# Attention between two expert layers on one core: tokens and queries of a batch made one batch ahead, the second half of the mix one score tile later and its values one batch later

## The reference

```python
x = x + 0.5 * ffn(layernorm(x))       # mixture of 16 experts, 4 chosen, and a shared one
x = x + attn(layernorm(x))            # causal attention, one head of width 128
x = x + 0.5 * ffn(layernorm(x))

# attn(x), mask -inf above the diagonal
Q = x @ Qw; K = x @ Kw; V = x @ Vw
scores = einsum('bqd,bkd->bqk', Q, K) / sqrt(128) + mask
return einsum('bqk,bkd->bqd', softmax(scores), V)
```

## Time and profile before

| | us |
|---|---|
| median of 3 runs | 779.87 (776.88 to 780.46) |
| the profiled execution | 777.23 |
| its span | 775.3 |
| first expert layer, up to the first score tile | 0 to 264 |
| attention with the start of the second layer | 264 to 545 |
| second expert layer | 545 to 775.3 |

### The profile page before, as it was taken

How to read it: one execution, slowest core, us unless ns; L and a number is a source line. 1 busy time by engine, 2 the same in 40 slices (tenths; PEclk the granted TensorE clock), 3 DMA queues, 4 the chain that set the end, 5 groups by cost and what they waited for, 6 DMA issues and landing times.

```text
span 775.3 us, 15281 instructions
## 1 busy us (share of the span) xinstructions
PE 666.4 (86%) x3395; PEld 516.1 (67%) x3395; DVE 591.0 (76%) x2650; ACT 548.4 (71%) x1138; POOL 537.9 (69%) x427
## 2 busy tenths in 40 slices
PE   5789999999999868667686676766999999999997
PEld 4567777777777646546565565655777777777775
DVE  5999898898898756564665575894888988998863
ACT  3589988988987754644545554443888889889885
POOL 3488998988998564444345353541798999989885
PEclk9999999999999968987789877787999999999999
DMA  9767577577577053434445433276388687687673
GB/s 253 164 145 169 115 163 164 123 160 157 129 163 148 1 96 69 85 68 81 80 64 83 80 57 72 47 134 138 68 172 172 144 186 166 153 177 164 148 171 92
DMA packets 129306, 97.31 MB, mean 126 GB/s; under 512 B 80992, under 2 KB 94960, under 8 KB 129264
## 3 DMA queue, kind: packets, MB, share of 16 engines
q1 hardware_dynamic: 127056, 96.24, 60.0%
q10 hardware_dynamic: 2208, 0.59, 0.4%
HBM read 72.70 MB, written 5.24 MB: 101 GB/s over the span
## 4 chain that ended last, share of the span: by engine, by line
PE 25%; DVE 16%; issue 10%; DMA 7%; ACT 6%; POOL 2%; SPq 0%; DVEq 0%; POOLq 0%; ACTq 0%
PE psum L1272 6%; DMA wb<-scratch 6%; PE psum L1274 6%; PE psum L1273 6%; DVE raw_max L1155 4%; DVE zn L1173 2%; DMA scratch<-wT 1%; PE psum L1488 1%; PE psum L1489 1%; PE psum L1490 1%; DVE s_sb L1026 1%; DVE x_sb L1185 1%; ACT s_sb L526 1%; ACT z_hi L526 1%; ACT s_sb L704 1%
## 5 line engine op out<-in xcount | busy, mean ns | idle before, releaser
L416 POOL TENSOR_TENSOR shared_r<-shared,shared_r 128x512 fp32r<-128x512 f32 x256 | 326.7, 1297 | 66.6 <-ACT shared L596 64.6
L1026 DVE SCALAR_TENSOR_TENSOR s_sb<-psum,wb 128x512 f32<-128x512 f32 x256 | 175.3, 688 | 48.8 <-PE psum L1274 21.0
L595 ACT ACTIVATE shared_r<-s_sb 128x512 fp32r<-128x512 f32 x256 | 160.0, 625 | 45.4 <-DVE s_sb L1026 43.3
L596 ACT ACTIVATE shared<-s_sb 128x512 f32<-128x512 f32 x288 | 177.9, 619 | 18.8 <-DVE s_sb L1026 18.6
L503 POOL TENSOR_TENSOR shared<-s_sb,shared 128x128 f16<-128x128 f32 (+3 forms) x64 | 81.9, 1281 | 95.7 <-ACT shared L526 95.7
L1272 PE MATMUL psum<-x_hi,w_hi 128*128 128x512 f32 x288 | 128.7, 447 | 0.4 <-DVE s_sb L1026 0.4
L704 ACT ACTIVATE s_sb<-psum,nmax 128x128 f32<-128x128 f32 (+3 forms) x64 | 47.4, 741 | 113.0 <-DVE nmax L1158 113.0
L1272 PE MATMUL psum<-shared_r,w_hi 128*128 128x512 f32 x256 | 114.6, 448 | 1.2 <-POOL shared_r L416 1.1
L1273 PE MATMUL psum<-x_lo,w_hi 128*128 128x512 f32 x288 | 115.2, 400 | 0.0
L1274 PE MATMUL psum<-x_hi,w_lo 128*128 128x512 f32 x288 | 114.8, 398 | 0.0
L1273 PE MATMUL psum<-shared_r,w_hi 128*128 128x512 f32 x256 | 101.2, 395 | 0.0
(11 more groups left out here) (182 smaller groups left out, 1425.6 us busy)
## 6 DMA issues: line engine op xcount, KB each, us to landing
wb<-scratch SPq DMA_DIRECT2D x128, 512.0 KB, 8.2
out<-x_sb SPq DMA_DIRECT2D x16, 256.0 KB, 9.9
x_sb<-in_L_attn_x SPq DMA_DIRECT2D x4, 256.0 KB, 6.0
scratch<-wT SPq DMA_DIRECT2D x32, 32.0 KB, 1.9
w_raw<-in_L_ffn_W ACTq DMA_DIRECT2D x1, 512.0 KB, 5.5
w_raw<-in_L_ffn_W SPq DMA_DIRECT2D x1, 512.0 KB, 6.5
w_raw<-shared SPq DMA_TRANSPOSE x32, 2.8
wb<-shared SPq DMA_TRANSPOSE x32, 3.9
```

Source lines behind the costliest of these rows:

```text
L416: nc.gpsimd.tensor_tensor(g_lo[:, j % RING, :], g_f[:, j % RING, :], g_hi[:, j % RING, :].bitcast(F32), ALU.subtract).then_inc(F.glo_done, 1)
L595: nc.scalar.activation(g_hi[:, j % RING, :], s_sb[:, j % RING, :], ACT.Square)
L596: nc.scalar.activation(g_f[:, j % RING, :], s_sb[:, j % RING, :], ACT.Square).then_inc(F.sq_done, 1)
L1026: ins = nc.vector.scalar_tensor_tensor(s_, h_, 0.0, wb[:, u, c, :], ALU.max, ALU.mult)
```

## The change

- Tokens and queries of batch b+1, both halves, are made in batch b, at tiles 0 to 4, from `zn` that was normalised in batch b-1: the statistics of batch b+2 stand at tiles 2 and 4, mean and inverse root at 5, `normalise` at 6 and 7. Batch 0 does it for batch 1 at later tiles and does batch 2's as well.
- The banks for it are the second bank of each score pair, bank 1 for the first half and 3 for the second (and 5 for the first half's queries), which tiles 0 to 3 leave free. So tiles 4 and 5 of batches 1 to 6 wait until the next batch's queries were read.
- The 16-bit tokens have three buffers, the third in the gate buffer `wb`, and are made at tiles 2 and 3 for the next batch.
- Pair 2 of the mix moves from tile 2 to tile 3, pair 3 is cut in two, at tiles 5 and 6; its copy moves from tile 6 to 7 on ScalarE. `values` of the second half moves from tile 7 of the next batch to tile 0 of the one after, and its `finish` from tile 7 to tile 1.
- The wait for the routing's sigmoid before a transpose in batch 6 goes.

```diff
...
         zn = sb("zn", [P, QT, D])
-        zn16 = sb("zn16", [P, UN, 2, QT, D], F16)
+        zn16_own = sb("zn16", [P, 2, 2, QT, D], F16)
+        zn16_wb = wb[:, 0].rearrange("p c n -> p (c n)")[:, 0:QT * D].bitcast(F16).rearrange("p (s t d) -> p s t d", s=2, t=QT)
+        zn16 = [zn16_own[:, 0], zn16_own[:, 1], zn16_wb]
...
+        def prep_ps(b, half):
+
+            if b == 1:
+                return (misc_ps, u_ps[0])[half], (misc_ps, u_ps[0])[half]
+            z_home = psum[:, 1 + 2 * half, :]
+            return z_home, spare_ps if half == 0 and b < B - 1 else z_home
...
-                        if t < 2:
-                            z16_lo(b, b % UN, t)
+                        if b == 0 and t < 2:
+                            z16_lo(b, t)
+                        if b == 0 and t == 2:
+                            attention_inv(1)
+                        if t == 5 and b + 2 < B:
+                            attention_inv(b + 2)
                         prob_lo(b, t)
-                        if t == 2 and b + 1 < B:
-                            attention_inv(b + 1)
+                        if t in ((2, 3) if b > 0 else (4, 5)) and b + 1 < B:
+                            z16_lo(b + 1, t % 2)
                         start_behind(b, t)
...
                     sc.wait_ge(A.zn_done, 2 * b + half + 1)
-                    wait(sc, A.mix_done, 4 * (b - 1))
+                    wait(sc, A.mix_done, 4 * (b - 2))
                     ts = slice(half * HQ, (half + 1) * HQ)
-                    copy(zn16[:, u, 0, ts, :], zn[:, ts, :]).then_inc(A.z16hi_done, 1)
...
-                            if t < 2:
-                                z16_hi(b, u, t)
                             if t == 0 and b == 0:
                                 q_hi_copy(b, u, 1, q_ps)
+                            if t < 2 and b == 0:
+                                z16_hi(b, t)
                             if t == 1 and b > 0:
                                 uT_copy(b - 1, 0)
-                                z_hi_copy(b, u, 1, z_ps)
-                            if t == 3 and b > 0:
-                                q_hi_copy(b, u, 1, q_ps)
-                            if t == 6 and b > 0:
+                            if t == 7 and b > 0:
                                 uT_copy(b - 1, 1)
-                            if t == 6 and b + 1 < B:
-                                z_hi_copy(b + 1, 1 - u, 0, next_ps)
-                            if t == 7 and b + 1 < B:
-                                q_hi_copy(b + 1, 1 - u, 0, next_ps)
+                            if b + 1 < B:
+                                z_at, z16_at, q_at = ((0, 1), (2, 3), (3, 4)) if b > 0 else ((3, 4), (4, 5), (5, 6))
+                                if t in z_at:
+                                    z_hi_copy(b + 1, 1 - u, z_at.index(t), prep_ps(b + 1, z_at.index(t))[0])
+                                if t in q_at:
+                                    q_hi_copy(b + 1, 1 - u, q_at.index(t), prep_ps(b + 1, q_at.index(t))[1])
+                                if t in z16_at:
+                                    z16_hi(b + 1, z16_at.index(t))
...
-                                v.wait_ge(AT.fin_done, 2 * (B - 3))
+                                v.wait_ge(AT.fin_done, 2 * (B - 4))
...
-                            if t < 2 and b + 1 < B:
-                                stats(b + 1, t)
+                            if t == 1 and b > 1:
+                                finish(b - 2, u, 1)
+                            if t == 0 and b == 0:
+                                stats(1, 0)
+                                stats(1, 1)
                             if t == 1 and b == 0:
                                 q_lo_part(b, u, 1, q_ps)
-                            if t == 2 and b > 0:
-                                z_lo_part(b, u, 1, z_ps)
-                            if t == 2 and b + 1 < B:
-                                mean(b + 1)
-                                norm_eps(A, b + 1, a_mv, QT, 0, a_mv[:, :, 1], scale=Z_SCALE ** -2)
+                                mean(1)
+                                norm_eps(A, 1, a_mv, QT, 0, a_mv[:, :, 1], scale=Z_SCALE ** -2)
+                            if t in (2, 3) and b == 0:
+                                normalise(1, t - 2)
                             if t == 3 and b > 0:
-                                q_lo_part(b, u, 1, q_ps)
-                            if t == 4 and b > 0:
                                 finish(b - 1, 1 - u, 0)
-                            if t in (4, 5) and b + 1 < B:
-                                normalise(b + 1, 1 - u, t - 4)
-                            if t == 6 and b + 1 < B:
-                                z_lo_part(b + 1, 1 - u, 0, next_ps)
-                            if t == 7 and b + 1 < B:
-                                q_lo_part(b + 1, 1 - u, 0, next_ps)
-                            if t == 7 and b > 0:
-                                finish(b - 1, 1 - u, 1)
+                            if b + 1 < B:
+                                z_at, q_at = ((1, 2), (3, 4)) if b > 0 else ((4, 5), (6, 7))
+                                if t in z_at:
+                                    z_lo_part(b + 1, 1 - u, z_at.index(t), prep_ps(b + 1, z_at.index(t))[0])
+                                if t in q_at:
+                                    q_lo_part(b + 1, 1 - u, q_at.index(t), prep_ps(b + 1, q_at.index(t))[1])
+                            if b + 2 < B:
+                                if t in (2, 4):
+                                    stats(b + 2, t // 2 - 1)
+                                if t == 5:
+                                    mean(b + 2)
+                                    norm_eps(A, b + 2, a_mv, QT, 0, a_mv[:, :, 1], scale=Z_SCALE ** -2)
+                                if t in (6, 7):
+                                    normalise(b + 2, t - 6)
...
+                    finish(b - 1, 1 - u, 1)
...
                     if t % HQ == 0:
                         pe.wait_ge(A.qlo_done, 2 * b + t // HQ + 1)
+                    if t in (HQ, HQ + 1) and 0 < b < B - 1:
+                        pe.wait_ge(A.qlo_done, 2 * b + 2 + t - HQ + 1)
                     wait(pe, A.exp_done, QT * b + t - 1)
...
+                def mix(b, pair, part=None):
...
+                    if part != 1:
+                        for t in (first, first + 1):
+                            pe.wait_ge(A.pT_in[t % PR], 16 * (2 * b + t // PR + 1))
+                        if pair == 0:
+                            pe.wait_ge(A.z16lo_done, 2 * b + 2)
+                        if b == 0 and pair == 0:
+                            pe.wait_ge(A.qlo_done, 2 * UN)
+                        wait(pe, A.uT_done, 2 * (b - 1) + half + 1)
+                    z16 = zn16[b % 3]
                     end = (first % HQ + 2) * P
-                    for k in range(first + 2):
+                    for k in range(HQ if part == 1 else 0, HQ if part == 0 else first + 2):
                         q0 = (first % HQ) * P + max(0, k - first) * P
...
+                    if part != 0:
+                        ins.then_inc(A.mix_done, 1)
...
-                            if t == 0 and b > 0:
-                                mix(b - 1, 1 - u, 0)
-                                mix(b - 1, 1 - u, 1)
-                            if t == 1 and b > 0:
-                                pe.wait_ge(A.exp_done, QT * b)
-                                z_transpose(b, u, 1, z_ps)
-                            if t == 2 and b > 0:
-                                mix(b - 1, 1 - u, 2)
-                            if t == 3 and b > 0:
-                                values(b - 1, 0)
-                                q_product(b, u, 1, q_ps)
-                            if t == 5 and b > 0:
-                                mix(b - 1, 1 - u, 3)
-                            if t == 6 and b + 1 < B:
-                                if b == 0:
-                                    pe.wait_ge(FF[0].res_done, NG)
-                                if b == B - 2:
-                                    pe.wait_ge(N1.sig_done, 2)
-                                z_transpose(b + 1, 1 - u, 0, next_ps)
-                            if t == 7 and b + 1 < B:
-                                q_product(b + 1, 1 - u, 0, next_ps)
-                            if t == 7 and b > 0:
-                                values(b - 1, 1)
+                            if b + 1 < B:
+                                z_at, q_at = ((0, 1), ()) if b > 0 else ((3, 4), (5, 6))
+                                if t in z_at:
+                                    if b == 0 and t == 3:
+                                        pe.wait_ge(FF[0].res_done, NG)
+                                    wait(pe, A.exp_done, QT * b + t - 1 if b > 0 else 0)
+                                    z_transpose(b + 1, 1 - u, z_at.index(t), prep_ps(b + 1, z_at.index(t))[0])
+                                if t in q_at:
```

(29 more changed lines are left out.)

28 lines of the change are left out of this document (11 added, 17 removed).

## The result

| | before | after |
|---|---|---|
| median of the runs, us | 778.38 (775.64 to 780.46, 4 runs) | 757.76 (756.80 to 761.05, 4 runs) |
| span of the profiled execution, us | 775.3 | 755.0 |
| mean granted clock over the span | 0.931 | 0.949 |

The ratio after to before is 0.9745, 95% interval 0.9697 to 0.9792. It is just under the band from 758 to 771 to which the forecast gave its 0.47, and beside the time of rival (a), 756. The row of before has one run more than the table in Time and profile before.

The account below looks back on a forecast made before the run. The attention was taken as bound by waits, two serial ladders per batch. Savings of 6.7 + 1.6 + 5.9 - 0.5 = 13.7 us took 777.23 to 763.5; one microsecond added gave 764.5, range 751 to 777.

Parts of the forecast that it names:

- rival (a): Attention's middle batches: the short gaps leave the clock alone, period 28.5, total 756 us; chance 0.20.
- The walk of one batch from tile 4: Middle batch, tile 4 to next tile 4: 27.5 us at the high clock, 30.0 with clock terms, against 31.67 before.
- The ladder before tile 4: TensorE idled 3.08 us for the queries' late second half; the wait moves before tile 5, costing 4.2 us.
- both ladders before the next tile 0: Late queries, and tokens and queries of the next batch, held TensorE; removing them saves 6.0 us from tile 5.
- The 1.4 us for the drop at the new gap: Low clock behind the gap before tile 5 adds 1.7 to 2.5 us of TensorE time; 1.4 shows per batch.
- The 1.1 for the gaps between tiles 0 and 3: Clock price per batch of gaps of 1.9 us before the values and 1.6 before the query product; bounds 0 and 3.7.
- The last batch: Tile 4 of batch 6 to tile 4's maximum in batch 7: 36.6 us against 42.53, saving 5.9 (0 to 8).
- rival (c): Last batch: routing, not VectorE's preparation, sets it, so 5.9 us is not gained; 769 us, chance 0.10.
- The hand-over: After the attention: values and finish fall about 3.5 us later for TensorE, covered by its old 7.63 us transpose wait.
- (b): Attention's middle batches: both short gaps drop the clock, period 32.6, total 777 us, no change; chance 0.15 with (e).
- (d): Attention: the clock doesn't come back within a batch, 37 us a batch, total 798; 0.08 with other mishaps.
- (e): Attention: the moves only shift the ladder; if next tile 0 also waits 2 for VectorE, 774 us; 0.15 with (b).

Follow-up runs that it names:

- e2: Changed kernel with 40 unused matmuls behind tile 4 in batches 1 to 5, filling 2.40 us of the gap before tile 5; 755.12 us, ratio 0.9695.
- e8: e1 with normalisation halves at tile 7 and next tile 0, the first two mixes ahead of the transposes, and e7's edit; 734.41 us, ratio 0.9456.
- e1: Changed kernel with the copies of the next batch's queries one score tile earlier, at tiles 2 and 3; 741.59 us, ratio 0.9529.
- e9: e4 with the fourth mix cut over tiles 5 and 6; 751.75 us, ratio 0.9677.
- e11: e10 with the values of the second half put back to tile 7; 730.52 us, ratio 0.9399.
- e7: Changed kernel with batch 1's normalisation at tiles 3 and 4 of batch 0 in place of 2 and 3; 759.27 us, ratio 0.9776.
- e10: e8 without e7's move of batch 1's normalisation; 730.95 us, ratio 0.9404.
- e4: Changed kernel with mix, its copy, values and finish back at their old places, keeping only the preparation one batch ahead; 768.29 us, ratio 0.9871.

## Why the prediction was right, and where its size was off

**Mechanism.** The walk of one batch from tile 4 holds, point by point. The third column is the changed kernel's batch 3, the rows of the second view above; the last is the batch from 309.3 us in e2, where the clock is full throughout.

| from tile 4's start | walk, with its clock terms | measured | walk at the high clock | measured in e2 |
|---|---|---|---|---|
| tile 5 | 5.33 | 5.28 | 5.33 | 5.30 |
| next tile 0 | 11.9 + 1.4 = 13.3 | 14.42 | 11.9 | 11.88 |
| values | 17.5 + 1.4 = 18.9 | 18.81 | 17.5 | 17.04 |
| next tile 4 | 27.5 + 2.5 = 30.0 | 28.56; mean of four 28.13 | 27.5 | 26.79 |

The ladder before tile 4 went to tile 5, where the wait is as long as was forecast; nothing behind it filled the gap; and both ladders before the next tile 0 are gone. The low clock moves tile 0 by 2.5 us against e2's batch, but the values by 1.8, since a wait of 0.52 us for the normalised tokens, which e2's batch has behind tile 0, is gone. The values came where the walk put them, behind the inverse root, the normalisation, tile 7's maximum and the copy. That is how the forecast had it (1.7 to 2.5 us of TensorE time, 1.4 in the end). The normalisation was taken at 2.1; one batch has it at 2.38, the next at 1.12.

**The term that was mis-sized: the clock, in its second half.** The 1.4 us for the drop at the new gap is right: 1.3 by e2. The 1.1 for the gaps between tiles 0 and 3 was nothing: the gaps are there (1.71 and 1.57), and the clock stayed at 1.00 from 378 to 391 us. That is the condition of rival (a), and its mechanism is the one seen. A drop at these places does happen in other kernels, but none came near the bound of 3.7: 1.3 us in e2, 0.7 to 0.9 in e8, nothing in e1. Beside it the walk was 0.65 too long: 27.5 at the high clock, where e2's full-clock batches take 26.85. 1.1 and 0.65 and the 0.1 between 1.4 and 1.3 are the 1.9 us by which the period of 28.13 is better than 30.0, and four times that is the 7.4 us of the middle batches. By the last two columns the 0.7 of e2's batch lie behind tile 0: 0.4 up to the values and 0.25 from there to tile 4.

**The ends.** The last batch is the best sized term: 36.69 against 36.6. VectorE is busy 27.38 us of it against 26.1, so its waits are some 1.2 shorter than forecast, and the two errors cancel; rival (c), that routing sets it, is refuted. Batch 5 to 6 took 29.21 against 31.5: 1.9 of the difference is the period's, and against the measured period of 28.13 it is 1.1 longer, so most of the 1.5 us put on for the second stage's statistics was paid. The start lost 4.8 against 0.5. The first score tile's maximum stands 1.93 later than before, in a stretch that the change doesn't touch and within the spread of the runs (from 264.48 in e9 to 267.96 in e11). The rest, 2.9, is in batch 0: the maximum of tile 4 comes 5.5 us later behind that of tile 0 than before, and up to tile 4 of batch 1 only 2.8 of it are won back (2.7 us lost, counted by the maxima). The 4 us stand for the root was forecast, and is 3.05. Not in the walk was another normalisation in that batch, that of batch 2's first half behind tile 6. VectorE's row comes first, then GpSimd's:

```profile
288.95 4.86 DVE L1188 TENSOR_SCALAR zn<-x_sb,a_mv,a_rstd 128x128 f32<-128x128 f32 x4
```

```profile
287.27 1.64 POOL L408 TENSOR_TENSOR a_rstd<-a_mv,neg_half 128x8 f32<-128x8 f32 x1
288.87 1.64 POOL L513 TENSOR_TENSOR shared<-s_sb,shared 128x768 f16<-128x768 f32 x1
290.47 1.16 POOL L508 TENSOR_TENSOR zn<-zn 128x512 f16<-128x512 f32 x1
291.58 1.88 POOL L513 TENSOR_TENSOR shared<-s_sb,shared 128x896 f16<-128x896 f32 x1
```

Three GpSimd operations in a row kept it for 4.86 us. e7 shows that moving batch 1's normalisation doesn't mend this. e10, with batch 2's one tile later, takes 40.72 us from the first tile's maximum to tile 4 of batch 1, where the change takes 42.12 and the kernel before 39.39; but it has the earlier mixes too (e1's edit alone gives nothing there, 42.14), so how the 2.9 divides stays open. The hand-over is covered as forecast: TensorE waits 6.04 us for the copied half behind tile 7, and 3.38 where 7.63 stood before, and the end comes 1.2 us sooner behind batch 7.

```profile
498.11 2.08 PE L1528 MATMUL psum<-vw,s_sb 128*128 128x128 f32 x8 [6.04 <-ACT s_sb L540]
...
507.78 0.37 PE L1516 MATMUL psum<-wb,zn 128*128 128x256 f16 x1 [3.38 <-issue]
```

**Rivals.** (a) is nearest, 756 against 757.8, but its sum has a slip: with 1.1 taken off, the walk's own terms give a period of 28.9 and not 28.5, and some 759 us. Its mechanism was right, and the measured period of 28.13 is below either. (b) and (d) need a clock that falls again or stays down; e4, with the fourth mix uncut behind the gap, shows such a thing, 54 us at half in four batches. (e) is refuted by the tile 0 that waits for nothing.

**The step that held only for the whole change.** The walk named the place of each step but gave the late mix no value of its own: "its sum is unchanged". e4 and e9 show that its place matters for the parts: with the values at tile 7 and no cut, nearly all of the gain of the preparation is lost, at tile 6's maximum, at the values and in the clock. The total came out because the walk was made with all the edits in place.

## What to carry to other kernels

A ladder that is moved to a place where nothing can fill the wait is only half removed: put the producer a tile earlier than its consumer's neighbour, as e1 does by two indices for another 2%. Price a drop of the clock by the waits that stand behind it, not by its length or place alone: some 3.4 us at half cost nothing in e1, where a wait of 1.77 us took it up, and 0.7 to 0.9 in e8; some 7 us cost 1.3 in e2, and so did the drops of the changed kernel in the mean, one of 3.4 and three of 7 us. Before a long batch is put down to the clock, look whether something came late before the clock fell: of e2's 3.2 us, 1.9 did. When a change has several parts, walk each without the others too: here the smallest one, a cut in a mix, decides whether the largest pays.

## What the runs showed of the hardware

A normalisation of four instructions on VectorE takes 1.11 to 1.12 us alone. Beside GpSimd it takes the longer, the longer the two overlap: 1.59 us with 0.73 of overlap, 2.17 with 1.32, 3.04 with 2.45, 3.99 with 3.66, and 4.86 with 4.60 beside three operations in a row. The four instructions of that last one, each in a row of its own:

```profile
288.95 1.66 DVE L1188 TENSOR_SCALAR zn<-x_sb,a_mv,a_rstd 128x128 f32<-128x128 f32 x1
290.52 1.19 DVE L1188 TENSOR_SCALAR zn<-x_sb,a_mv,a_rstd 128x128 f32<-128x128 f32 x1
291.63 1.91 DVE L1188 TENSOR_SCALAR zn<-x_sb,a_mv,a_rstd 128x128 f32<-128x128 f32 x1
293.47 0.33 DVE L1188 TENSOR_SCALAR zn<-x_sb,a_mv,a_rstd 128x128 f32<-128x128 f32 x1
```

The Trainium skill, SBUF — State Buffer, section SBUF: two separate sides, has the port pair as an exclusive lock held for a whole instruction, and these rows agree. What they add is what a row of GpSimd operations does: the first three instructions end at 290.61, 291.71 and 293.54 us, each about 0.08 behind the end of a GpSimd operation (290.51, 291.63, 293.46), and the fourth, with nothing beside it, takes 0.33. One of them gets through at each boundary between two GpSimd operations, and the next one stands through the following operation.

The clock is not decided by one wait. It stood at 0.50 around the wait of 4.00 us before tile 5 in every middle batch of the changed kernel, and in batch 3 it had fallen before the wait was over (0.78 from 366.74 to 367.74 us, 0.50 in the next microsecond, tile 5 at 368.70). But in e1 the same matmul after the same wait, 2.76 us in one batch and 2.78 in the next, had the low clock once and the full clock once:

```profile
342.89 0.92 PE L1476 MATMUL psum<-ident,zn 128*128 128x128 f32 x4 [2.76 <-DVE zn L1188]
...
368.46 0.63 PE L1476 MATMUL psum<-ident,zn 128*128 128x128 f32 x4 [2.78 <-DVE zn L1188]
```

```profile
342.90:346.70 3.80, 3.80 (x22) 2.94 (x22) 2.56 (x8) 2.57 (x4) 0.23 (x1) 0.55 0.83 156
368.50:372.30 3.80, 2.23 (x22) 1.91 (x22) 2.52 (x8) 2.60 (x4) 0.26 (x1) 1.00 1.15 114
```

Which waits bring a drop isn't settled by these runs. Waits of 1.56 us and less had none in e10's four batches, and the same waits had three drops in e8's.
